# Mixing each sample in its own half of TensorE's rows, with x transposed and taken through its spectrum one base chunk earlier and the bias added last on GpSimd

## The reference, cut to what matters

```python
# 1. per-sample adapter, then autocorrelation over the 1024 columns
Bx = einsum('bni,bri->bnr', x, B[ids]);  y = einsum('bnr,bor->bno', Bx, A[ids])
corr = irfft(rfft(y) * conj(rfft(y)))
weights, delay = top_k(corr, 6)                       # int(log(1024)) = 6 delays for each row
x = x + sum_k softmax(weights)[k] * roll(y, -delay[k])
# 2. per-sample 64 x 64 mixing of the rows, then a base matrix with a routed low-rank part
x2 = einsum('bct,bcd->bdt', x, W[condition])          # each sample has its own 64 x 64 matrix
logits = x2 @ W_router.T;  top 2 of 8 experts, renormalised
out = x + x2 @ W_base.T + b_base + 2 * lora(x2)
```

## Time and profile before

| | |
|---|---|
| median of 3 runs | 855.38 us (853.22 to 855.9) |
| profiled execution, its own time | 851.39 us |
| span of its instructions | 849.6 us |
| mean granted TensorE clock | 0.969 |
| PE busy | 788.3 us, 93% of the span |
| DVE, POOL, ACT busy | 655.4, 510.5 and 328.2 us |
| DMA | 193.48 MB, mean 228 GB/s |

### The profile page before, as it was taken

One profiled execution on the slowest core, in us unless ns is written; L12 is line 12 of the kernel. 1 busy time (PEld: TensorE's weight loads), 2 busy tenths in 40 slices (PEclk: granted clock), 3 DMA queues, 4 the chain that ended last, 5 costly groups with the idle time before them and its releaser, 6 DMA issues.

```text
span 849.6 us, 14441 instructions
## 1 busy us (share of the span) xinstructions
PE 788.3 (93%) x4828; PEld 657.8 (77%) x4828; DVE 655.4 (77%) x1387; ACT 328.2 (39%) x624; POOL 510.5 (60%) x447
## 2 busy tenths in 40 slices
PE   2967799999999999999999999999999999999897
PEld 2755678788878888788888888788878887877786
DVE  1256688988878787988878787988888788888952
ACT  3455344333543444333543444333533442333211
POOL 0123476757678766757677766757677664566621
PEclk9866799999999999999999999999999999999999
DMA  7769577887877888888877888887877877875521
GB/s 208 221 181 246 197 243 255 261 221 222 267 252 220 242 260 252 262 221 237 252 240 243 234 261 247 263 225 220 271 233 248 239 230 227 262 237 191 189 84 50
DMA packets 65661, 193.48 MB, mean 228 GB/s; under 512 B 13548, under 2 KB 23180, under 8 KB 62484
## 3 DMA queue, kind: packets, MB, share of 16 engines
q0 software_dynamic: 23040, 83.90, 33.9%
q1 hardware_dynamic: 31988, 72.93, 30.2%
q10 hardware_dynamic: 10560, 35.75, 10.8%
HBM read 117.82 MB, written 50.33 MB: 198 GB/s over the span
## 4 chain that ended last, share of the span: by engine, by line
PE 55%; POOL 15%; DVE 13%; issue 7%; DMA 5%; ACT 4%; SPq 1%; ACTq 1%; POOLq 0%; DVEq 0%
PE o_ps L502 27%; PE h_ps L640 5%; PE x_ps L526 5%; DMA y_d<-y 4%; PE c_ps L502 4%; POOL rolled L1266 3%; POOL turn L1289 3%; POOL eo L1293 3%; POOL row L1250 3%; PE t_ps L575 2%; PE t_ps L598 2%; PE x_ps L508 2%; ACT eo_hi L888 2%; PE x_ps L629 2%; POOL eo L1292 2%
## 5 line engine op out<-in xcount | busy, mean ns | idle before, releaser
L1266 POOL DMA_INDIRECT rolled<-y_d,off x160 | 203.9, 1274 | 218.2 <-DVE row L1073 105.2
L1073 DVE SCALAR_TENSOR_TENSOR row<-rolled,weight,row 128x1024 f32<-128x1024 f32 x160 | 222.1, 1388 | 10.2 <-DMA rolled<-y_d,off 3.9
L502 PE MATMUL o_ps<-wt_hi,x_hi 128*128 128x512 f32 x512 | 219.3, 428 | 0.0
L502 PE MATMUL o_ps<-wt_hi,x_lo 128*128 128x512 f32 x512 | 203.2, 397 | 0.0
L502 PE MATMUL o_ps<-wt_lo,x_hi 128*128 128x512 f32 x512 | 202.9, 396 | 0.0
L502 PEld LDWEIGHTS o_ps<-wt_hi,x_hi 128*128 128x128 f32 x512 | 97.4, 190 | 22.2 <-issue 4.6
L502 PEld LDWEIGHTS o_ps<-wt_hi,x_lo 128*128 128x128 f32 x512 | 96.4, 188 | 23.4
L502 PEld LDWEIGHTS o_ps<-wt_lo,x_hi 128*128 128x128 f32 x512 | 96.9, 189 | 15.7
L1250 POOL TENSOR_TENSOR row<-row,bias 128x1024 f32<-128x1024 f32 x32 | 77.7, 2427 | 16.3 <-PE x_ps L629 15.8
L849 ACT ACTIVATE turn<-t_ps 128x512 f32<-128x512 f32 x64 | 35.0, 596 | 101.5 <-PE t_ps L575 101.5
L1289 POOL TENSOR_TENSOR turn<-turn 128x256 f32<-128x256 f32 x64 | 71.7, 1141 | 2.6
(11 more groups left out here) (156 smaller groups left out, 1505.6 us busy)
## 6 DMA issues: line engine op xcount, KB each, us to landing
y_d<-y ACTq DMA_DIRECT2D x64, 512.0 KB, 3.6
row<-in_x SPq DMA_DIRECT2D x32, 512.0 KB, 7.7
out<-row SPq DMA_DIRECT2D x32, 512.0 KB, 6.1
adapter<-g_hi SPq DMA_DIRECT2D x62, 256.0 KB, 6.5
adapter<-g_lo SPq DMA_DIRECT2D x31, 256.0 KB, 6.7
r<-in_L_cond_A SPq DMA_DIRECT2D x60, 64.0 KB, 3.5
r<-in_L_cond_B SPq DMA_DIRECT2D x56, 64.0 KB, 5.9
rolled<-y_d,off POOLq DMA_INDIRECT x160, 7.1
```

Of the source, the lines that this page charges most:

```text
L502: last = pe.matmul(dst, a, b, start=start and n == 0, stop=stop and n == len(todo) - 1)
L1073: dve.scalar_tensor_tensor(rows[:, :], from_buffer[:, :], weight[:, n:n + 1], rows[:, :], ALU.mult, ALU.add).then_inc(sum_step, 1)
L1266: pool.indirect_dma_start(out=rolled[at % RB][:, :], out_offset=None, in_=y2_d[u], in_offset=bass.IndirectOffsetOnAxis(ap=off[s % 2][:, n: ...
```

## The change

Six things change, all on the order or the form of instructions; the transfers stay.

1. `mixed`: for each of the eight column chunks the one matmul with 128 rows and 128 columns becomes two, one for each sample: 64 rows of the array (0 to 63, or 64 to 127), 128 weight columns, 64 moving columns. Sample 0 goes to the first 512 columns of `x_ps`, sample 1 to the second.
2. `mixed_out` and `mixed_low` copy by samples instead of by column halves. So `project` and base chunk 0 need both copies, where before each needed the first half to start.
3. PE: `x_transposed` stands between the projection and base chunk 0; `b_times_x`, `bx_repeated`, `spectrum` and `adapter_out` each come one base chunk earlier. `h_transposed` stays.
4. POOL: `bias_added` moves from between the gathers 0 to 2 and the powers to behind gathers 3 and 4.
5. DVE: `bx_masked` and `stack_low` come ahead of the sum that each stood behind, and the second half of the router comes ahead of `weights` and `add_y`.
6. ACT: the copies of the adapters' preparation come behind those of the running tile.

```diff
             def mixed(t):
                 pe.wait_ge(mix_in[t % NMIX], (t // NMIX + 1) * 32)
                 pe.wait_ge(sum_step, SUMS * t + SUMS)
+                rows, w = row[t % NROW], mix[t % NMIX]
                 for c in range(KC):
-                    last = pe.matmul(x_ps[:, c * P:(c + 1) * P], row[t % NROW][:, c * P:(c + 1) * P], mix[t % NMIX][:, :],
-                                     start=True, stop=True)
-                    if c % 4 == 3:
-                        last.then_inc(x2_mm, 1)
+                    for b in range(SPT):
+                        q, at = slice(b * C, (b + 1) * C), b * 512 + c * C
+                        last = pe.matmul(x_ps[:, at:at + C], rows[q, c * P:(c + 1) * P], w[q, q],
+                                         start=True, stop=True)
+                        if c == KC - 1:
+                            last.then_inc(x2_mm, 1)
...
             def project(t):
                 if t > 0:
                     pe.wait_ge(ht_l, t)
+                pe.wait_ge(x2_f, 2 * t + 2)
                 for c in range(KC):
-                    if c % 4 == 0:
-                        pe.wait_ge(x2_f, 2 * t + 1 + c // 4)
...
             def base(t, c):
-                if c % 4 == 0:
-                    pe.wait_ge(x2_l, 2 * t + 1 + c // 4)
+                if c == 0:
+                    pe.wait_ge(x2_l, 2 * t + 2)
...
             def mixed_out(m):
-                for h in range(2):
-                    act.wait_ge(x2_mm, 2 * m + 1 + h)
-                    act.activation(x2[:, 4 * h:4 * h + 4, :].rearrange("p k r -> p (k r)"),
-                                   x_ps[:, h * 512:(h + 1) * 512], ACT.Copy).then_inc(x2_f, 1)
-                    act.activation(x2_hi[:, 4 * h:4 * h + 4, :].rearrange("p k r -> p (k r)"),
-                                   x_ps[:, h * 512:(h + 1) * 512], ACT.Copy).then_inc(x2_h, 1)
+                for b in range(SPT):
+                    act.wait_ge(x2_mm, 2 * m + 1 + b)
+                    of = x_ps[:, b * 512:(b + 1) * 512].rearrange("p (k r) -> p k r", k=KC)
+                    act.activation(x2[:, :, b * C:(b + 1) * C], of, ACT.Copy).then_inc(x2_f, 1)
+                    act.activation(x2_hi[:, :, b * C:(b + 1) * C], of, ACT.Copy).then_inc(x2_h, 1)
...
                 if has(last):
                     gather(last, (u - 1) % U, range(3))
-                if has(t):
-                    bias_added(t)
                 if has_attn(s):
                     powers(s)
                 if has(last):
                     gather(last, (u - 1) % U, range(3, NSEL))
+                if has(t):
+                    bias_added(t)
```

More of the change, by code:

```diff
@@ L690, in slot @@
                     project(t)
+                if attn:
+                    x_transposed(s, 0)
+                    x_transposed(s, 1)
                 for c in range(KC):
@@ L697, in slot @@
                         fold_transposed(g)
-                    if c == 0 and attn:
-                        x_transposed(s, 0)
-                        x_transposed(s, 1)
+                    if c == 1 and attn:
+                        b_times_x(s, u, i)
                     if c == 2 and attn:
-                        b_times_x(s, u, i)
-                    if c == 2 and u == 0 and prep and ffn:
-                        pe.wait_ge(x2_l, 2 * t + 2)
+                        bx_repeated(s)
                     if c == 2 and u == 0 and prep:
+                        if ffn:
+                            pe.wait_ge(x2_l, 2 * t + 2)
                         a_transposed(g)
                     if c == 3 and attn:
-                        bx_repeated(s)
+                        spectrum(s, u, i)
                     if c == 3 and u == 2 and prep:
@@ L711, in slot @@
                     if c == 4 and attn:
-                        spectrum(s, u, i)
+                        adapter_out(s, u)
                     if c == 4 and u == 2 and prep:
@@ L716, in slot @@
                         b_transposed(g)
-                    if c == 5 and attn:
-                        adapter_out(s, u)
                     if c == 5 and ffn:
@@ L901, in slot @@
                 attn, prep = has_attn(s), has_group(g)
+                if attn:
+                    x_out(s, t)
                 if prep and u == 2:
                     fold_out(g)
-                if attn:
-                    x_out(s, t)
                 if has(last):
@@ L911, in slot @@
                                    accum_out=rsum[:, :]).then_inc(rexp_out, 1)
+                if attn:
+                    stack_high(s)
+                    square(s)
                 if prep and u == 0:
@@ L914, in slot @@
                 if attn:
-                    stack_high(s)
+                    y_copy(s)
                 if prep and u == 2:
                     a_high(g, u, i)
-                if attn:
-                    square(s)
-                if prep and u == 2:
                     spectrum_high(g)
@@ L923, in slot @@
                     b_out(g)
-                if attn:
-                    y_copy(s)
                 if has(t):
@@ L1136, in mixed_low @@
             def mixed_low(m):
[L1137 to L1141, removed]
+                for b in range(SPT):
+                    dve.wait_ge(x2_h, 2 * m + 1 + b)
+                    low(x2_lo[:, :, b * C:(b + 1) * C],
+                        x_ps[:, b * 512:(b + 1) * 512].rearrange("p (k r) -> p k r", k=KC),
+                        x2_hi[:, :, b * C:(b + 1) * C]).then_inc(x2_l, 1)
             def slot(s, u, i):
@@ L1149, in slot @@
                     router(t, 0)
+                if attn:
+                    bx_masked(s)
                 if has(m):
                     add_rolled(m, 3)
+                if attn:
+                    stack_low(s)
+                if has(m):
                     add_rolled(m, 4)
-                if attn:
-                    bx_masked(s)
+                if has(t):
+                    router(t, 1)
                 if has(last):
@@ L1157, in slot @@
                     add_y(last)
-                if attn:
-                    stack_low(s)
-                if has(t):
-                    router(t, 1)
                 if has(last):
```

## The result

The changed kernel takes 878.47 us (median of 4 executions, 874.46 to 886.07), the kernel before 855.64 (853.22 to 856.09): ratio 1.0283, 95% interval 1.0205 to 1.0361, slower. The profiled execution took 881.05 us, its span is 879.2, against 851.39 and 849.6.

A forecast was written before the change was run, and what follows sets the result against it. PE, busy 93%, sets the pace; the bias and gather 1 loops add 1.1 us to each of 7.25 periods (+8), the end -1: 851.39 becomes 858.4, or 862 against the median. Range 841 to 886.

The forecast's parts named there:

- The mixing: On PE: the split passes run side by side in two row halves, +0.25 us a slot on 1.70.
- cost nothing: Copies by samples: needing both halves adds no time, as transposes of x (some 0.8 us) cover base chunk 0.
- My -1 for the end: End of the run: a single wait of 2.6 us in front of `h_transposed`, counted as a gain of 1 us.
- PE's steps one chunk up: On PE: 1.5 us more room ahead of the correlation, so its waits for `eo_lo` and `h_transposed`'s for `hc` go.
- B + 8.85: B is the start of base chunk 0; POOL was forecast to start the powers 8.86 us after it.
- The 0.82 us a slot for `hc`: PE's assumed loss ahead of `h_transposed` in a slot of kind 1, from 8.2 us over 10 waits.
- The bias loop: POOL's late bias delays the output sum and `x_lo` on DVE, so base chunk 0 starts at 22.8 us (kind 3).
- Kind 2: Slot with over 4 us of transforms behind the spectrum, said to hide the late bias: 26.65 us.
- The loop through gather 1: Mask, a sum and gather 1's landing delay `ht_lo`, so the experts on PE lose 1.4 us in kind 1.
- My forecast for kind 1: Slot length of 23.65 us: 23.05 from the wait for `ht_lo`, and another 0.6 from a later mask.
- The rival "the bias in front of `eo_lo`": POOL's bias holds `eo_lo`, correlation up to 2.4 us later in three of four slots: 906 us, chance 0.03.
- The rival "all waits go": PE's waits vanish and none replace them: 836 us in full, 846 half way; chance 0.35, at least in part.

The follow-up runs named there:

- e4: The changed kernel with the whole mixing of before, one 128 x 128 matmul a chunk, copies and waits by column halves: 866.45 us, ratio 1.0151 to the kernel before.
- e10: The changed kernel with the whole mixing of before and POOL's bias ahead of gathers 0 to 2: 836.58 us, ratio 0.9827 to the kernel before.
- e13: The changed kernel with only POOL's bias moved, to ahead of gathers 0 to 2: 847.33 us, ratio 0.9939 to the kernel before.

## Why the prediction was right in sign and too small in size

**The mixing** was right: 1.93 us, forecast 1.95, with the halves side by side. What was left out are its other prices. Behind the split mixing the correlation takes 1.82 us and the projection 1.93 (starts at 400.71, 402.53 and 404.46); in e4 they take 1.75 and 1.86 (393.63, 395.38, 397.24). I had called the waits for both copies "cost nothing" with the transposes of x as cover. In a slot that holds nearly. In the drain there is no correlation and nothing else between mixing and projection, and it costs 3.6 and 3.4 us. My -1 for the end was the wrong sign: from base chunk 0 of the first full slot to that behind the last, the profiled execution is 23.2 us longer than before, and outside of it 6.5.

**PE's steps one chunk up** did what was said: `hc` is no wait, the powers begin at B + 8.85. (The 0.82 us a slot for `hc` was a misreading: the ten waits include the single one of 2.6 us, which stands in the drain; the other nine are 0.62 on average.) The two kernels with the bias in front show that the room is real: a period of e10 (22.41 + 22.63 + 22.41 + 26.43 from base chunk 0 to base chunk 0) is 93.88 us, and e13's some 94.5.

**The bias loop** was the right mechanism, and it is shown: moving the bias alone gives 31 us. Its terms were too small. From the powers' start to gather 3 I took 6.80; in the period above it is 7.53 in kind 3 and 7.56 in kind 1. Two gathers took 2.24 us in the slot of kind 3 (forecast 2.29), but 3.03 in that of kind 0, in which gather 3 takes 1.76 instead of 0.96. So kind 3 is held until 23.6 instead of 22.8 and kind 0 until 23.8 (23.6). Kind 2 was rightly called hidden, its base chunk 0 has no wait; that it takes 26.94 and not 26.65 is the split's price, since e13, in which the bias holds nothing, has 26.91 there and e10, with the whole mixing, 26.43.

**The loop through gather 1** was wrong as a price. The waits it names are there, but with 0.32, 0.50 and 0.33 us ahead of the experts in the kinds 3, 0 and 1 of the period shown above, where I had PE lose 1.4 in kind 1. The term that was off is the landing: I took 8.2 us from the issue of gather 1, and in this slot of kind 1 it is 6.2. My forecast for kind 1, 23.65 against 23.69 measured, came out for the wrong reason, which is luck: the bias loop gives it (8.86 to the powers, 7.56, 2.31 and 2.38 to the end of the bias, 2.58 to base chunk 0). What the loop costs, it costs in few slots. At 257.49 gather 1 landed 7.6 us after its issue, and DVE and then PE show what follows:

```profile
265.17 1.86 DVE L1072 SCALAR_TENSOR_TENSOR row<-rolled,weight,row 128x1024 f32<-128x1024 f32 x1 [1.32 <-DMA rolled<-y_d,off]
```

```profile
267.28 0.50 PE L502 MATMUL o_ps<-bs_hi,ht_hi 128*128 128x512 f32 x1 [1.83 <-DVE ht_lo L1013]
```

Behind this stop PE ran for 10.2 us at a granted clock of 0.50, and the slot of kind 1 lasted 28.4 us, not 23.7.

**The rival "the bias in front of `eo_lo`"** had been given 0.03 and a place in three of four slots. It does occur, in one slot of the profiled execution and with an extra price that was not in it. In the changed kernel at 496 us, POOL and then DVE:

```profile
496.19 2.73 POOL L1250 TENSOR_TENSOR row<-row,bias 128x1024 f32<-128x1024 f32 x1
```

```profile
496.62 2.98 DVE L1013 TENSOR_TENSOR eo_lo<-eo,eo_hi 128x640 fp32r<-128x640 f32 x1
```

`eo_lo` (0.8 us elsewhere) takes 2.98, the correlation waits, and correlation and projection then run at a granted clock of 0.67. This slot is 29.2 us from base chunk 0 to base chunk 0, not 26.9. It doesn't take the bias, though: in e10 POOL's `g_lo`, which then stands where the bias stood, does the same once, and that slot takes 27.6 us instead of 26.4:

```profile
475.98 2.74 POOL L1243 TENSOR_TENSOR g_lo<-r,g_hi 128x1024 fp32r<-128x1024 f32 x1
```

```profile
476.43 2.99 DVE L1012 TENSOR_TENSOR eo_lo<-eo,eo_hi 128x640 fp32r<-128x640 f32 x1
```

No step of mine had a clock in it.

The sum, for the profiled executions: of the 23.2 us in the full slots 7.25 periods of +2.68 are 19.4, and the 3.8 left are the two stops (4.7 and 2.3) less what a few other slots are shorter; with the 6.5 outside, 29.7. Forecast were 8, 0 and -1. The medians are only 22.8 us apart: the profiled execution of the changed kernel is 2.6 above its median, that of the kernel before 4.2 below.

The rival "all waits go" gave 836 us as its full price and 846 as the half way. With the split mixing in it, and the bias in front, e13 came to 847.3; e10, whose mixing is whole, to 836.6.

## What to carry to other kernels

An instruction that nobody waits for early, moved to the end of its engine's queue, is on the path as soon as something late waits for it: look first for the place where its engine already stands idle behind its inputs, here the start of the slot, and put it there. (In the kernel before, without the rest of the change, this place was not tried.) Two orders whose instructions hold each other up (here POOL's bias and DVE's sums) have to be tried together: DVE's new order cost 109 us with the bias ahead of the powers, and gave 29 with the bias last. When a wait for a half becomes a wait for the whole, look at the first and the last rounds of the loop too, where the work that covers it is missing.

## What the runs showed of the hardware

- **A large POOL instruction can hold a DVE one until it ends, however small that is.** Beside the bias (2.4 us) an eight-column operation took 3.09 us and a sum with y 4.13. Both had begun 0.65 us ahead of the bias, while POOL was still issuing the gather in front of it. In e13 two POOL instructions without a gap between them, the second one the bias, made `eo_lo` take 5.87 (DVE, then POOL):

```profile
196.52 5.87 DVE L1013 TENSOR_TENSOR eo_lo<-eo,eo_hi 128x640 fp32r<-128x640 f32 x1 [0.30 <-ACT eo_hi L890]
```

```profile
197.04 2.36 POOL L1244 TENSOR_TENSOR g_lo<-r,g_hi 128x1024 fp32r<-128x1024 f32 x1
199.34 2.35 POOL L1250 TENSOR_TENSOR row<-row,bias 128x1024 f32<-128x1024 f32 x1
```

  Operations that read PSUM were not held (`x_lo`, MAX8 in e10). The Trainium skill (SBUF — State Buffer, SBUF: two separate sides) tells of an exclusive lock on a shared port pair, taken for a whole instruction and not a share of the bandwidth. By that the traces agree: the held instruction ends with POOL's, or its own length later.
- **A stop of PE can cost as much again in clock, or more, and need not.** After 1.68 us without work the granted clock was 0.55 for the next 3.74 us; after 2.99 us it was 0.59 for 8.4; after 2.62 it was 0.50 for 9.3. By these figures the clock took some 1.7, 3.4 and 4.7 us (an estimate: the stretch times the share not granted). But in the kernel before PE also stood for 2.62 us, ahead of `h_transposed` at 805.08 us, and the granted clock was 1.00 in the stop and in the 10 us behind it. What decides between the two is not shown here.
- **Two halves of the rows load and multiply side by side only if neighbours in the program use different halves**: 1.93 us for 32 passes in pairs, 3.32 in turn, and 1.70 for the 16 whole passes that do the same work.
